# Recurrent attention block with gated projection on Trainium2: a ScalarE copy, an output half, an ffn product and the weight tables change their place in the order

## The reference, cut to what matters

```
xn = layernorm(x)                                        # x: 4 x 1024 x 1024, f32
h  = rmsnorm(xn) * qkv_norm_w
q, k, v = h @ quant(qkv_w).T                             # weights in {-1,0,1} * scale
# per head (16 heads of 64), over chunks of 128 tokens, state S (64 x 64):
scores = (q k^T) * mask ;  intra = scores @ v
cross  = (q * lam_t) @ S ; o = (intra + cross) / 8
S      = lam_T * S + (k * lam_rev)^T @ v
out    = rmsnorm(rmsnorm(o) * norm_w) * proj_norm_w @ quant(proj_w).T
g      = silu(xn @ quant(ffn_w).T + bias)
result = x + out * g
```

## Time and profile before

| | |
|---|---|
| median of three runs | 1396.1 us |
| the profiled execution | 1395.49 us, span 1394.2 us |
| TensorE matmuls | 1329.7 us busy, 95% of the span |
| TensorE weight loads | 843.8 us, 61% |
| VectorE | 951.4 us, 68% |
| ScalarE | 582.2 us, 42% |
| GpSimd | 653.2 us, 47% |
| mean granted TensorE clock | 0.989 of full speed |

### The profile page before, as it was taken

One profiled execution on the slowest core, in us unless ns is written; L12 is line 12 of the kernel. 1 busy time (PEld: TensorE's weight loads), 2 busy tenths in 40 slices (PEclk: granted clock), 3 DMA queues, 4 the chain that ended last, 5 costly groups with the idle time before them and its releaser, 6 DMA issues.

```text
span 1394.2 us, 25938 instructions
## 1 busy us (share of the span) xinstructions
PE 1329.7 (95%) x10409; PEld 843.8 (61%) x10409; DVE 951.4 (68%) x1489; ACT 582.2 (42%) x1139; POOL 653.2 (47%) x532
## 2 busy tenths in 40 slices
PE   5999999989999999999999999999999999999998
PEld 2577677655646557465664646557466574756655
DVE  7896477694766768577684776758666685766835
ACT  6883243343434434343343434434343343434421
POOL 1523875762534545345450554545345352654333
PEclk9999999999999999999999999999999999999999
DMA  9521303003030030301203030030301203020000
GB/s 364 209 92 61 99 2 114 16 17 114 1 126 4 18 112 17 113 1 52 78 16 113 2 119 12 16 114 5 125 2 44 86 17 114 1 85 15 32 31 31
DMA packets 33432, 90.32 MB, mean 65 GB/s; under 512 B 10529, under 2 KB 10785, under 8 KB 33314
## 3 DMA queue, kind: packets, MB, share of 16 engines
q1 hardware_dynamic: 33024, 88.65, 18.2%
q10 hardware_dynamic: 290, 0.02, 0.0%
HBM read 71.85 MB, written 16.81 MB: 64 GB/s over the span
## 4 chain that ended last, share of the span: by engine, by line
PE 85%; DVE 6%; POOL 3%; ACT 2%; issue 2%; DMA 1%; SPq 0%; ACTq 0%; DVEq 0%; POOLq 0%
PE ring L747 18%; PE ring L880 15%; PE ring L706 12%; PE ring L680 11%; PE ring L732 11%; PE att_ps L784 4%; PE att_ps L830 3%; PE att_ps L834 3%; PE ring L796 2%; PE att_ps L811 2%; DVE y L1209 1%; PE ring L759 1%; POOL sq L2182 1%; PE ring L655 1%; DMA raw<-in_ffn_w 1%
## 5 line engine op out<-in xcount | busy, mean ns | idle before, releaser
L747 PE MATMUL ring<-b_lo,qkv_q 128*128 128x256 f16 x1216 | 268.2, 272 | 0.0
L747 PE MATMUL ring<-b_hi,qkv_q 128*128 128x256 f16 x1216 | 268.2, 273 | 0.0
L880 PE MATMUL ring<-proj_q,o_hi 128*128 128x512 fp8e4 x496 | 188.2, 379 | 3.6 <-DVE o_lo L1422 3.6
L880 PE MATMUL ring<-proj_q,o_lo 128*128 128x512 fp8e4 x496 | 188.0, 379 | 0.0
L2204 POOL TENSOR_TENSOR xt<-xt,gate_even 128x512 f32<-128x512 f32 x58 | 88.9, 1543 | 160.7 <-DVE gate_even L1442 159.5
L2178 POOL TENSOR_TENSOR sq<-sq,cols 128x1024 f32<-128x1024 f32 x29 | 55.0, 1897 | 161.6 <-DVE b_lo L1254 153.3
L747 PEld LDWEIGHTS ring<-b_hi,qkv_q 128*128 128x128 fp8e4 x1216 | 120.2, 99 | 15.6
L747 PEld LDWEIGHTS ring<-b_lo,qkv_q 128*128 128x128 fp8e4 x1216 | 118.9, 98 | 15.8
L1442 DVE SCALAR_TENSOR_TENSOR gate_even<-ring,wscale,gate_even 128x512 f32<-128x512 f32 x58 | 43.5, 750 | 118.8 <-PE ring L880 118.5
L2138 POOL TENSOR_TENSOR gate_even<-gate_even,bias 128x512 f32<-128x512 f32 x14 | 19.7, 1408 | 216.8 <-ACT gate_even L1819 216.8
L2182 POOL TENSOR_TENSOR sq<-sq 128x1024 f32<-128x1024 f32 (+1 forms) x58 | 109.4, 1886 | 4.5
(11 more groups left out here) (257 smaller groups left out, 3294.6 us busy)
## 6 DMA issues: line engine op xcount, KB each, us to landing
xt<-in_x SPq DMA_DIRECT2D x62, 512.0 KB, 8.1
out<-xt SPq DMA_DIRECT2D x31, 512.0 KB, 3.1
raw<-in_qkv_w SPq DMA_DIRECT2D x24, 512.0 KB, 15.8
y<-in_x_turned SPq DMA_DIRECT2D x14, 512.0 KB, 6.7
y_odd<-in_x_turned SPq DMA_DIRECT2D x14, 512.0 KB, 7.5
raw<-in_ffn_w SPq DMA_DIRECT2D x8, 512.0 KB, 9.7
norm_rows<-norm_out SPq DMA_DIRECT2D x14, 256.0 KB, 5.9
raw<-in_proj_w SPq DMA_DIRECT2D x6, 512.0 KB, 4.6
```

The source lines that it names most:

```text
L747: ins = pe.matmul(ring[:, b, e * BT:(e + 1) * BT], qkv_q[:, cb, o:o + P], part[:, cb, :], start=(cb == 0 and part is b_hi), stop=(cb == NC ...
L880: ins = pe.matmul(ring[:, b, :], part[:, cb, :], proj_q[:, cb, cs], start=(cb == 0 and k == 0), stop=(cb == NCB - 1 and k == 1))
```

## The change

The work is the same; only the order is changed, with one wait added.

- TensorE: the second half of the previous block's output projection goes from behind k's p6 to between k's p5 and p2. In chunk 0 of blocks 3 to 15 ffn's p6 goes from ahead of the outputs to behind the state update.
- ScalarE: `high_part` of S4 goes behind the seed and `begin_k(i, 1)`.
- VectorE: `go_on_z12`, which takes ffn's p6, goes behind `weight_o` and `add_state`.
- GpSimd: v's T1 goes ahead of two output additions, T2 and T4 stand together ahead of `decay_q`, T3 goes ahead of `output_scale(1, 0)`, which now is ahead of `decay_state`. k's T1, T2, T4 go ahead of the last output addition of block 1 (T1 with a new wait for the last low sum of b), and T3 from the start of block 3 to block 2.

```
@@ attention_by_tokens (TensorE)
                     turn_k(i, 1)
-                    product(i, "p6")
...
                 if c == 0:
+                    product(i, "p6")
                     product(i, "p2")
@@ tensor_program, blocks 3 to 15
                 k_product(i, "p5")
+                project_out(i - 1, 1, 1)
                 k_product(i, "p2")
                 k_product(i, "p6")
-                project_out(i - 1, 1, 1)
@@ attention_by_tokens (VectorE)
-                    go_on_z12(i)
                     weight_o(i, 0, 0)
                     weight_o(i, 0, 1)
                     add_state(i, 0)
+                    go_on_z12(i)
@@ scalar_program, blocks 3 to 15
-                for name in Y_SUMS:
-                    high_part(i, name)
+                high_part(i, "S1")
+                high_part(i, "S3")
+                high_part(i, "S2")
                 begin_k_bank(i)
                 begin_k(i, 1)
+                high_part(i, "S4")
@@ sum_k_weights (GpSimd)
                 if name == "T1":
...
+                    pool.wait_ge(s_bslo, of_b_sum(2, "S4"))
@@ attention (GpSimd)
                 if c == 1:
                     sum_squares(i, 0)
+                if (i, c) == (1, 1):
+                    sum_v_weights("T3")
+                    output_scale(1, 0)
                 if not is_first(g) and not is_last(g):
                     decay_state(i, c)
                 if c == 0:
                     if i == BY_TOKENS - 1:
-                        for name in ("T1", "T2"):
-                            sum_k_weights(name)
+                        sum_k_weights("T3")
...
-                    if i == BY_TOKENS - 1:
-                        sum_k_weights("T4")
                     if i == 1:
-                        for name in ("T1", "T2"):
+                        for name in ("T2", "T4"):
                             sum_v_weights(name)
...
-                    if i == 1:
-                        sum_v_weights("T4")
                 else:
-                    output_scale(i, 0)
-                    if i == 1:
-                        sum_v_weights("T3")
+                    if i != 1:
+                        output_scale(i, 0)
@@ gpsimd_program, the blocks
                         for name in ("T1", "T2", "T4", "T3"):
                             sum_weights(name)
-                    if i == BY_TOKENS:
-                        sum_k_weights("T3")
+                        sum_v_weights("T1")
                     add_out(i - 1, 1, 0)
+                    if i == BY_TOKENS - 1:
+                        for name in ("T1", "T2", "T4"):
+                            sum_k_weights(name)
                     add_out(i - 1, 1, 1)
```

## The result

The changed kernel takes 1341.26 us (median of 4 runs, 1340.99 to 1341.53), the kernel before 1395.98 us (1395.75 to 1396.25) in runs on the same chip: a ratio of 0.9608, 95% interval 0.9591 to 0.9625, or 54.7 us less. Forecast were 1342.7 us, 1339 to 1352.

What follows compares the result with a forecast made beforehand. TensorE, 85% of the chain, was taken as the bound. 36.1 (stops) + 16.5 (clock) + 0.8 (tables) = 53.4 us off 1395.49 gives 1342.1, plus 0.6 for the median 1342.7 us; range 1339 to 1352.

Steps and rivals of the forecast that it cites:

- The stops, 36.1 us: Blocks 3 to 15: TensorE's waits before k's p2 for ScalarE's seed all go, 36.1 us; bounds 33 to 36.1.
- Either half of the edit alone would nearly do: Before k's p2, stop 2.54 us: S4's copy moved alone gains 2.2 us, the output projection moved alone gives 3.45.
- The clock, 16.5 us: k's p2 and p6 in blocks 3 to 15: no lower TensorE clock after stops, 16.5 us gained; bounds 0 and 16.5.
- The tables, 0.8 us: Block 1: v's T3 on GpSimd moved off the b_lo group, 0.8 us gained; bounds 0 and 0.8.
- The 1 us that I allowed for k's tables: Block 2: k's T1, T2, T4 meet the centring of block 3's y; taken as 0, bounds 0 and 1 us lost.
- ffn's p6, 0: ffn's p6 moved behind the state: same eight matmuls on TensorE's path, no new wait, taken as 0.
- the bound of 2.3: Upper bound for moving ffn's p6: TensorE's three waits for GpSimd's squares gone, 2.3 us gained.
- The centring, cost 0 by a margin of 0.7 us: VectorE's centring of next y, 6.8 us long, still lets v's second addition precede v's p4 by 0.7 us; cost 0.
- that possibility: VectorE's four centring instructions may be shorter once GpSimd's decays, running earlier, are out of their way; no size given.
- the rival that a new wait of 1 us arises in each block: Centring waits for its transfer or p7 for its base, 1 us in 12 blocks, some clock drops kept: 1355 us; chance 0.12.
- the slower one: y's transfer queues behind more traffic and lands late; at 12 us after issue, 1408 us; chance 0.02.
- The seed: Block 6, ScalarE: waits for the first gating alone, starts about 562.05, ends 562.65, 3.7 us before p2.

Runs made afterwards that it cites:

- the half alone: Kernel before with only the second output half moved between k's p5 and p2, S4's copy still ahead of the seed: 1346.32 us.
- the copy alone: Kernel before with only ScalarE's copy of S4 moved behind the seed and k's second begin: 1342.63 us.
- The run with six stops: Changed kernel with the earlier order of S4's copy and the output half back in blocks 4, 6, 8, 10, 12, 14: 1362.81 us.
- the run of the faster version: Changed kernel, in blocks 4, 8, 12 GpSimd's first sum of squares between q's two decays and the output scale earlier: 1338.53 us.
- with y late: Changed kernel with y's two transfers issued behind the three loads of x of the same stage: 1362.93 us.
- y late with the old and the new tables: Kernel before with y's transfers behind three loads of x: 1404.35 us; the same with GpSimd's tables also moved as in the change: 1391.73 us.

## Why the prediction was right

The forecast was 53.4 us; the profiled executions differ by 54.1 and the medians by 54.7. From block 3 on the 53.2 us are the forecast 36.1 and 16.5 and some 0.6 for ffn's p6, which I had put at 0. Ahead of block 3 there are 0.5 us for the tables, put at 0.8, and 0.4 of start-up, which no term of mine covers. The small errors of the tables and of p6 stand on opposite sides, so that the total came so near is in part luck; the two large terms are not.

*The stops, 36.1 us.* Right: the wait is gone in every block, block 3 too. "Either half of the edit alone would nearly do" holds with its exception: the half alone leaves 2.3 us in block 3. The 2.2 us of the 2.54 that I gave the copy alone were too few by my own rows: the seed starts 564.83 - 562.05 = 2.8 us earlier, and the run shows no stop left.

*The clock, 16.5 us.* Right. The mean granted clock is 1.000 against 0.989, TensorE's busy time is 17.7 us lower (1312.0 against 1329.7), and the 32 matmuls from p2 to p7 take 6.91 us in block 6, their length at full clock. The run with six stops shows that in these blocks a drop needs a stop and that a stop doesn't always bring one; why this one and not that stays open.

*The tables, 0.8 us.* Right in place, a little too large in size: the group of low parts of b takes 1.13 us in place of 1.94, but TensorE's wait behind it is only 0.5 shorter; the 1.35 in the medians and the 0.9 in the spans hold start-up besides. On the kernel before they were worth 5.4 us in the medians and 4.4 by the rows, since there the seed stood behind the collision; the parts don't add up. The 1 us that I allowed for k's tables beside the centring was not lost, though they do meet. GpSimd's T4 of k and VectorE's first centring instruction in block 2, in time, in the changed kernel:

```profile
235.98 3.83 POOL L2135 TENSOR_TENSOR k_sum_last<-qkv_q,k_sum 128x2048 fp8e4<-128x2048 fp8e4 x1
```

```profile
237.26 3.62 DVE L1164 TENSOR_TENSOR y<-y,norm_rows 128x1024 f32<-128x1024 f32 x1 [2.27 <-DMA y<-in_x_turned]
```

It takes 3.62 us where 1.23 is its length alone, so it ends 2.4 us late, 1.07 us behind T4's end at 239.81, close to the 2 us which the rule on the shared ports (the Trainium skill, "SBUF — State Buffer", "SBUF: two separate sides") let me expect; the trace agrees. The other three are longer too, beside an output addition and decays of GpSimd; the last one is

```profile
245.33 2.17 DVE L1166 TENSOR_TENSOR y_odd<-y_odd,norm_rows 128x1024 f32<-128x1024 f32 x1
```

so that the four end 10.2 us after they began. TensorE shows no wait for it. Where two tables stood beside the centring, the price was a wait of 4.7 us and the slow matmuls behind it.

*ffn's p6, 0.* 0.65 us in fact (0.75 by the traces), without any wait; the bound of 2.3 was not reached, since the squares wait for GpSimd's own queue, as the run of the faster version shows.

*The centring, cost 0 by a margin of 0.7 us.* The cost was right, the margin was wrong. VectorE waits 4.20 us for y, as forecast, but the four instructions take 4.9 us in all and not 6.8:

```profile
561.92 1.23 DVE L1164 TENSOR_TENSOR y<-y,norm_rows 128x1024 f32<-128x1024 f32 x1 [4.20 <-DMA y<-in_x_turned]
563.18 1.23 DVE L1166 TENSOR_TENSOR y<-y,norm_rows 128x1024 f32<-128x1024 f32 x1
564.33 1.22 DVE L1164 TENSOR_TENSOR y_odd<-y_odd,norm_rows 128x1024 f32<-128x1024 f32 x1
565.58 1.22 DVE L1166 TENSOR_TENSOR y_odd<-y_odd,norm_rows 128x1024 f32<-128x1024 f32 x1
...
569.94 0.75 DVE L1230 SCALAR_TENSOR_TENSOR arena<-ring,wscale,arena 128x512 f32<-128x512 f32 x1 [0.98 <-PE ring L706]
```

GpSimd's decays now end at 556.94, before y lands. In the kernel before they stood beside the centring, which began at 578.39:

```profile
578.84 4.01 POOL L2165 TENSOR_TENSOR arena<-arena,lam_T 64x512 f32<-64x512 f32 x2
```

I named that possibility and did not price it. The busy times of VectorE and GpSimd, 16.7 and 17.7 us lower than before, fit such meetings gone, though no row adds these up. The last row of the centring's view is at the same time the reason for the cost 0: the second addition waits for TensorE, not TensorE for it. The slack is 2.5 us, not 0.7, so the rival that a new wait of 1 us arises in each block, and the slower one, needed a landing 2 us later still than I reckoned. The mechanism of the rival is real: with y late it cost 21.7 us.

*The seed.* Forecast to end at 3.7 us before p2; ScalarE in time, block 6:

```profile
545.74 0.58 ACT L1789 ACTIVATE ring<-ring 128x512 f32<-128x512 f32 x1 [0.48 <-DVE gate_even L1442]
546.62 0.69 ACT L1799 ACTIVATE gate_odd<-ring,wscale 128x512 f32<-128x512 f32 x1 [0.30 <-PE ring L732]
547.95 0.63 ACT L1751 ACTIVATE sum_hi<-y 128x512 f16<-128x512 f32 x1 [0.64 <-DVE y L1209]
```

It ends at 546.32, 3.7 us before p2 at 550.03, released by the gating alone. S4 comes later than I wrote, after k's first copy, and harms nothing.

## What to carry to other kernels

Read what a late operation on the path stands behind on its own engine: here a helper waited for data that its successor didn't need, and moving it behind its successor gave by itself 53 of the 55 us with no work removed (cover alone, the other half, gave 50). Price a stop of TensorE at its length and the slow matmuls behind it, by the rows of each stop. When a stop goes, look for the slack that it gave to others (here a transfer with 2.5 us in hand), and judge each part of an edit from the kernel it lands in: the tables were worth 5.4 us with the stop there and 1.35 without. When such a difference is about 1 us, compare the traces stretch by stretch: here up to 1.5 us lay in the start-up of single executions.

## What the runs showed of the hardware

- Equal stops of 2.54 us are followed by TensorE's lower clock in seven of twelve cases, and in three of six when every second block has one. In five kernels with the same twelve stops (before, the tables alone, ffn's p6 alone, and y late with the old and the new tables) it is seven, seven, seven, eight and eight, never at the same set of stops. What chooses them no run shows.
- VectorE's centring instruction, 1.23 us alone, took 4.73 and 4.85 us beside GpSimd's T1 and T2 of k, and these took 4.69 where T4 took 3.83: both engines' instructions can get longer in such a meeting, not VectorE's alone. The ends alternate, at 241.89 (VectorE), 245.57, 246.65, 250.34 and 251.43 us: VectorE's two end 1.1 us behind GpSimd's, and GpSimd's 3.7 behind VectorE's, each about its own length alone.
- y's transfer of 512 KB lands 5.9 us after its issue in block 6; with one load of x issued ahead of it, 6.7 us, with three, 8.4 us.
